# A graph network layer's gathered products: three parts in one product of 192 columns

## What is computed

```
mean = segment_sum(x[src], dst) / max(degree, 1)                      # round 0
h    = relu([x, mean] @ W_fc + b_fc) + x @ W_res + b_res
x1   = layernorm(x + h)
h1   = relu(segment_sum(x1[src] @ Wm1 + bm1 + edge_attr @ We1 + be1, dst) + x1 @ Ws1 + bs1)   # round 1
h2   =      segment_sum(h1[src] @ Wm2 + bm2 + edge_attr @ We2 + be2, dst) + h1 @ Ws2 + bs2    # round 2
out  = layernorm(x1 + h2)
```

## Time and profile before

| | us |
|---|---|
| median of 3 runs | 5270.2 |
| lowest and highest | 5269.23, 5283.6 |
| the profiled execution | 5251.91 |
| its span, first to last instruction | 5250.1 |
| PE busy in the span | 3801.8 (72%) |
| DVE busy | 2493.0 (47%) |
| POOL busy | 2248.7 (43%) |
| ACT busy | 1577.5 (30%) |

### The profile page before, as it was taken

One profiled execution on the slowest core, in us unless ns is written; L12 is line 12 of the kernel. 1 busy time (PEld: TensorE's weight loads), 2 busy tenths in 40 slices (PEclk: granted clock), 3 DMA queues, 4 the chain that ended last, 5 costly groups with the idle time before them and its releaser, 6 DMA issues.

```text
span 5250.1 us, 120588 instructions
## 1 busy us (share of the span) xinstructions
PE 3801.8 (72%) x39993; PEld 3184.3 (61%) x39993; DVE 2493.0 (47%) x6331; ACT 1577.5 (30%) x2106; POOL 2248.7 (43%) x2698
## 2 busy tenths in 40 slices
PE   0257677778877777577777688877887687787774
PEld 0245566665555555466667677766776576676763
DVE  6377666766655656477776422222222222222224
ACT  0133355555555555477775200000002000000000
POOL 6321233334333434222222555555555655555552
PEclk9589989988898998899999888888888888888886
DMA  2702234344444444466664677776775777676774
GB/s 94 79 34 84 111 138 164 141 161 167 164 166 165 165 165 165 135 189 188 188 187 112 198 248 259 253 243 237 268 249 171 248 248 246 232 248 238 250 244 133
DMA packets 331871, 968.01 MB, mean 184 GB/s; under 512 B 151102, under 2 KB 244417, under 8 KB 274402
## 3 DMA queue, kind: packets, MB, share of 16 engines
q1 hardware_dynamic: 272086, 873.36, 47.5%
q0 software_dynamic: 59712, 93.77, 7.5%
HBM read 706.74 MB, written 263.39 MB: 185 GB/s over the span
## 4 chain that ended last, share of the span: by engine, by line
PE 54%; issue 19%; DVE 10%; another core or an unknown queue 4%; ACT 4%; DVEq 3%; POOL 3%; DMA 2%; ACTq 0%; SPq 0%; POOLq 0%
PE ps L1014 38%; PE ps L1035 9%; PE ps L1006 4%; DVE union L729 3%; DVE union L832 2%; ACT union L1315 2%; PE ps L1079 2%; ACT abuf L1297 2%; DVE abuf L843 1%; DVEq L409 1%; POOL msg L1166 1%; DVEq L843 1%; POOL union L1120 1%; DMA msg<-y_tab,idx 0%
## 5 line engine op out<-in xcount | busy, mean ns | idle before, releaser
L1166 POOL DMA_INDIRECT msg<-y_tab,idx x1776 | 1829.5, 1030 | 2135.4 <-ACT idx L1277 1615.5
L1014 PE MATMUL ps<-union,abuf 128*128 128x192 bf16 x14504 | 1567.0, 268 | 359.2 <-issue 318.8
L1014 PEld LDWEIGHTS ps<-union,abuf 128*128 128x128 f16 x14504 | 1345.9, 107 | 545.6 <-issue 489.0
L729 DVE TENSOR_TENSOR union<-lane,union 128x512 f16<-128x512 f16 (+3 forms) x2048 | 985.3, 531 | 492.0 <-PE ps L1035 265.8
L1297 ACT ACTIVATE abuf<-ps 128x784 f16<-128x784 f32 x1184 | 923.6, 822 | 884.0 <-PE ps L1035 596.5
L1035 PE MATMUL ps<-union 128*128 128x196 f16 (+2 forms) x4096 | 712.8, 309 | 411.1 <-ACT abuf L1297 169.7
L1014 PE MATMUL ps<-early,abuf 128*128 128x195 bf16 x7350 | 806.7, 264 | 0.0
L1014 PEld LDWEIGHTS ps<-early,abuf 128*128 128x128 f16 x7350 | 708.2, 106 | 69.8 <-issue 18.3
L1035 PEld LDWEIGHTS ps<-union 128*128 128x128 f16 x4096 | 337.3, 111 | 641.1 <-ACT abuf L1297 366.1
L1277 ACT ACTIVATE idx<-src_g 128x8 int32 (+1 forms) x222 | 46.0, 208 | 2117.1 <-PE ps L1006 1891.8
L1079 PE MATMUL ps<-union 128*64 128x128 f32 x7280 | 479.2, 278 | 173.3 <-ACT union L1315 157.8
(11 more groups left out here) (229 smaller groups left out, 1192.2 us busy)
## 6 DMA issues: line engine op xcount, KB each, us to landing
abuf<-a_dram SPq DMA_DIRECT2D x296, 1568.0 KB
a_dram<-abuf SPq DMA_DIRECT2D x74, 3136.0 KB
union<-in_edge_attr_dram SPq DMA_DIRECT2D x728, 160.0 KB, 2.4
msg<-y_tab,idx POOLq DMA_INDIRECT x1776
y_tab<-union SPq DMA_DIRECT2D x28, 336.0 KB, 2.9
y_tab<-early SPq DMA_DIRECT2D x7, 682.5 KB, 9.8
abuf<-x_pad SPq DMA_DIRECT2D x7, 448.0 KB
abuf<-x_pad SPq DMA_DIRECT2D x14, 224.0 KB, 2.9
```

Of the source, the lines that this page charges most:

```text
L729: return V.tensor_tensor(to.rearrange("p s (c u) -> p s c u", u=2), lanes.unsqueeze(1).to_broadcast([P, HB, width // 2, 2]), codes[:, whic ...
L1014: last = nc.tensor.matmul(ps[:, bank, 0:3 * width_of[r]], abuf[:, buffer, hi * P:(hi + 1) * P], ycols[r][:, hi, :], start=hi == 0, stop=hi ...
L1166: pool.indirect_dma_start(msg[:, s, 0:3 * width_of[r]], None, y_tab[r], bass.IndirectOffsetOnAxis(ap=idx[:, s:s + 1], axis=0)).then_inc(ga ...
```

## The change

In rounds 1 and 2 a gathered tile's three parts go through PE in one product of 192 columns that writes them side by side; the eight tiles of a set fill four banks, two tiles in each (`wide_tile_ps`, banks 0 to 3). Both sets use the same four banks, so g_multiply(j) now waits for `gred` of the other set. DVE sums the three parts of all eight tiles in one reduction into a new SBUF tile `part_g`, frees the banks (`gred`) right after it, and adds the eight tiles to their blocks from `part_g`. Round 0 stays as it is.

```
@@ in the tiles and semaphores
+        part_g = sb("part_g", [P, G, D])
+        g_red = sems("g_red", 2)
@@ beside tile_ps
+        def wide_tile_ps(k):
+
+            return ps[:, k // 2, k % 2 * 3 * D:(k % 2 + 1) * 3 * D]
@@ VectorE, g_add
                     bs = load_blocks((it * 2 + j + 1) * (G // 4), G)
                     dve.wait_ge(gsum[r][j], it + 2)
+                    if r:
+                        V.tensor_reduce(part_g[:, :, :].rearrange("p (b k) d -> p b k d", k=2),
+                                        ps[:, 0:G // 2, 0:6 * D].rearrange("p b (k c d) -> p b k d c", k=2, c=3),
+                                        AX.X, ALU.add).then_inc(g_red[r - 1], 1)
+                        dve.wait_ge(g_red[r - 1], it * 2 + (j + 1))
+                        dve.sem_inc(gred[r][j], 1)
+                        for k in range(G):
+                            to = feat[:, bass.ds(bs[k], 1), :]
+                            V.tensor_tensor(to, to, part_g[:, k:k + 1, :], ALU.add).then_inc(s_add[r], 1)
+                            dve.wait_ge(s_add[r], before + (k + 1))
+                        return
@@ TensorE, g_multiply
                     pe.wait_ge(gathered[r][j], (it + 1) * (16 * G))
 
-                    pe.wait_ge(gred[r][j], it + (1 if r else 1 + j))
+                    if r:
+                        pe.wait_ge(gred[r][1 - j], it + (1 + j))
+                        for k in range(G):
+                            s = j * G + k
+                            last = nc.tensor.matmul(wide_tile_ps(k), hot_g[:, s, :], msg[:, s, 0:3 * D], start=True, stop=True)
+                        last.then_inc(gsum[r][j], 1)
+                        return
+                    pe.wait_ge(gred[r][j], it + (1 + j))
```

## The result

| | before | after |
|---|---|---|
| median | 5276.9 us (4 runs) | 5366.1 us (4 runs) |
| lowest and highest | 5269.2, 5287.4 | 5350.9, 5373.6 |
| span of the profiled execution | 5250.1 | 5358.3 |

The ratio is 1.0164, with a 95% interval of 1.0131 to 1.0197: the changed kernel is 89 us slower. The forecast was 5197 us and the range ended at 5278; the measured time lies above both.

A forecast was written before the change was run, and what follows sets the result against it. PE was taken to be starved of instructions while POOL gathers. Terms -68 - 12 + 3 + 4 = -73 us on the profiled 5251.9 give 5179, plus 18.3 to the runs' median: 5197 us; range 5115 to 5278.

The forecast's parts named there:

- What bounds the kernel: Dense loops of rounds two and three: PE's instructions come slowly while POOL gathers; 420 us of "issue" idle.
- (1): PE: a half step has 212 instructions, not 244; two thirds of the gathered product's holes go, 68 us gained (0 to 144).
- rival one: No change, 5265 us: the starved time is POOL's; gathered product's idle falls, dense product's rises as much; chance 0.18.
- (2): PE columns: eight wide products cost nearly what 24 narrow ones do; gain 12 us, bounds 0 and 75.
- the much faster rival: Narrow products cost a fixed 62 ns each at any clock, so 117 us gained in place of 12: 5092 us; chance 0.04.
- (3): VectorE: reduction of 1.8 us a half step delays the marking; costs 3 us, plus 4 at the rounds' ends.
- Covered by 0.9 us: Marking ends 7.7 us after the gathered product; the fastest PE needs it at 8.6 us, so the delay is mostly hidden.
- (4): PE's new wait for the other set's reduction before writing the shared banks: nothing; POOL, ACT and SP get nothing new.
- The rival through POOL: Additions with both operands in SBUF hold up POOL's gathers, 1.8 us a half step: +193, 5463 us; chance 0.06.
- both kinds occur: Half steps where removed gathered-product slots save holes, and others where they follow the last gather and win nothing; middle taken, 68 us.

The follow-up runs named there:

- e1: Kernel before, with POOL's indirect gathers of the second and third round left out: 4424.2 us, ratio 0.840.
- e3: Changed kernel with the wide product but no reduction; each addition takes only the first part, from PSUM: 5185.6 us, ratio 0.985.
- e2: Changed kernel with three narrow products of 64 columns per tile written into the wide layout, VectorE's side as changed: 5394.0 us, ratio 1.026.
- e4: Changed kernel with 32 small products ahead of the second round's loop, moving PE's later instructions in the program: 5366.4 us, ratio 1.020.
- e17: Changed kernel, marking reads one operand from PSUM, reduction kept, additions read the first part from PSUM; fourth chip: 5484.6 us, ratio 1.042.
- e18: Changed kernel, marking reads one operand from PSUM, no reduction, additions read two SBUF operands; fourth chip: 5372.1 us, ratio 1.021.
- e9: Changed kernel with one operand of the marking read from PSUM in place of SBUF: 5506.7 us, ratio 1.043.
- e5: Changed kernel with an extra VectorE operation of 0.76 us ahead of each marking: 5304.3 us, ratio 1.009.
- e13: e3 with e9's marking (one operand from PSUM), on the third chip, where the kernel before takes 4211.6: 4160.4 us, ratio 0.987.
- e16: Kernel before with POOL resting once a set, after the fourth gather; third chip: 4326.3 us, ratio 1.025.
- e10: Kernel before with one operand of the marking read from PSUM in place of SBUF: 5438.9 us, ratio 1.031.

## Why the prediction was wrong

**What bounds the kernel: right.** PE starved of instructions while POOL gathers: e1 takes the gathers away, and with them all "issue" idle.

**(1) Fewer instructions: the size of the gain came out, the way to it did not.** The holes in front of the changed kernel's gathered product fell by 87 us (68 forecast), and e3, which has PE's side alone, gains 75. But e3's own rows show another way:

```profile
L1045 PE MATMUL ps<-union,abuf 128*128 128x192 bf16 x14504 | 1526.0, 261 | 409.5 <-issue 363.7 <-DMA abuf<-a_dram 28.1
L1030 PE MATMUL ps<-msg,hot_g 128*128 128x192 bf16 x1184 | 179.4, 294 | 44.0 <-issue 41.9
```

Against the earlier trace rows the "issue" idle in front of the gathered product fell by 60 us, and that in front of the dense product rose by 45: 15 us less in all, where 68 were forecast. That is three quarters of rival one, which said that the dense product takes the holes over. What e3 gains is PE's busy time: 41 us in the dense product and 24 in the gathered one, at a granted clock of 0.87 in both rounds in place of 0.85 and 0.84. The sum had 12 us for that, and no term for the clock. That e3 comes out near the forecast is luck. Only where the supply is slow anyway do the holes themselves fall with the instructions: 553 us in e2, 521 in e4.

**(2) Columns: right at an equal clock.** The last half step's eight wide products take 0.84 us, against 0.92 for 24.

```profile
5287.75 1.48 PE L1023 MATMUL ps<-msg,hot_g 128*128 128x192 bf16 x8
5289.03 9.02 PE L1038 MATMUL ps<-union,abuf 128*128 128x192 bf16 x98
5297.89 0.84 PE L1023 MATMUL ps<-msg,hot_g 128*128 128x192 bf16 x8
```

The one before it, at 5287.75, takes 1.48 us, and 24 narrow ones took 1.48 to 1.49: eight wide and 24 narrow cost the same at either clock, so the narrow ones have no fixed price, and the much faster rival falls.

**(3) The reduction: its duration right, its price wrong. This is the step that failed.** 1.76 us against 1.8, the marking 7.7 us after the product as worked out, and nobody waits for it. "Covered by 0.9 us" was true and beside the point. I asked only who waits for VectorE, and not what VectorE's work does to others while it runs. The sum put 3 + 4 us on VectorE's side; e4 less e3 is 181 us. It costs in two ways. It moves the marking's phase against POOL's gathers: POOL starts one every 1.26 us, the first 1.13 us after the gathered product's end; before, the marking ran typically from 4.66 to 5.89 us and met the gather that starts at 4.91 early; after, from 6.49 to 7.72, it meets the one at 7.43 in its last 0.3 us only, or misses it. And it lowers PE's supply in the free half steps (e17 and e18). In the two loops e4 takes 177 us more than e3. e17 less e18 puts 79 of them on the supply. e4 has 40 held half steps fewer than e3 (57 against 97), at 1.9 us each some 77 us. The remaining 21 are open. That the two parts add up in this way is argued and not measured by itself.

**(4) The waits: right**, none of them shows.

**The rival through POOL** had the right parts the wrong way round. I weighed it on the earlier trace rows, the addition with both operands in SBUF beside a gather of 0.95 us, and held that against the rule of the Trainium skill ("SBUF — State Buffer", SBUF: two separate sides), that a VectorE operation with two SBUF inputs locks a port pair. In those rows the gather starts 0.07 us before the addition. The count above shows that only a gather that *starts* during such an operation is held; e9, with one operand in PSUM, has none. So in this the trace agrees with the rule, and my reading of the earlier trace rows was at fault. The other way round nothing is held: the marking at 4845.61 starts during a gather and takes its usual 1.23 us, as do all 102 that do so in the changed kernel (1.22 or 1.23 us). The new additions, the ones that this rival was about, do hold gathers, by next to nothing: of 298 gathers that start during one, the 59 that start 0.05 to 0.09 us after its start are longer, by 0.05 us at most and some 1.2 us together. And the hold is no cost here: taking it away costs 141 and 170 us.

**What the prediction had before it.** The earlier trace rows hold a gather of 1.80 us, none, and PE's pieces once it has run dry are 4 to 11 products in the one and 2 to 5 in the other. I put the two down as "both kinds occur" and took the middle for the gain, without asking what makes a half step one kind or the other. They are not the two kinds: the earlier trace rows is one of the ten half steps in which POOL pauses for 2.22 us, and it is beside this pause that PE ran 98 dense and 17 gathered products without a hole. Asking what makes the kinds would have shown that 1.8 us on VectorE aren't free.

**Open.** Why a held gather lets PE's instructions through, and why the reduction slows them, no row shows. VectorE's own instructions come late too: the "issue" idle in front of the marking is 48.4 us in the changed kernel and 3.3 in the one before, 60.1 in e17 and 0.5 in e18. Nor does a row show why the third round lost more meetings than the second (17 held against 47, in e4 23 against 34), why e5, with more held half steps than the kernel before, is still slower than it (its held ones get some 8 instructions per us, not 13), what POOL does in its pauses of 2.22 us, or why PE is not starved at all on one of the chips.

## What to carry to other kernels

When an engine idles on "issue" while another engine issues indirect gathers, treat the phase of everything that runs beside the gathers as part of the time: a longer VectorE step that nobody waits for can cost more than the change saves elsewhere (here +180 us against -75). Split a change that touches two engines into its halves before judging it, and sort the half steps of the trace by kind before taking a mean over them. When a half of the change gives the forecast time, look whether it does so by the forecast term. Try a rest for the engine that gathers, and measure it on more than one chip: it gave 3.6% against the kernel before on one, with the wide products, and cost 2.5% on another, without them.

## What the runs showed of the hardware

- On every chip but one PE ran out of instructions in most half steps some 5 us after gathering began (in half of the changed kernel's 5.1 to 5.3 us, after 116 to 121 instructions; before 4.7 to 6.9 us, after 109 to 136), and then got 2 to 13 per us. On that one, e13 to e16 have no such hole in front of the dense product, and the kernel before takes 4212 us, against 5259 to 5277. e1 reached 4424 us on a starving chip by leaving the gathers out.
- A gather that starts while VectorE runs an operation with two SBUF operands lasts until some 0.8 us after that operation's end (1.98 us at 3524.22, with the marking ending at 3525.38); one that started before it isn't held (0.95 us at 4845.50), nor is one that starts during an operation that reads PSUM (163 during the reduction, 0.96 us at most).
- Every 112 gathers POOL paused 2.22 us after a gather with no wait of its own, in both kernels and in e9, e10, e17 and e18.
- Adding work made the changed kernel faster three times, against its 5366 us on another chip: 0.76 us on VectorE a half step (-62 us), 0.42 us on ACT (-88 us), 0.95 us on POOL (-284 us).
